# Four heads of attention on four row groups of TensorE, with 19 full-size matmuls as a bridge between projections and attention

## What is computed

```python
h = _layernorm(x) * (1 + ca) + sa
x = x + ga * attention(h)        # 16 heads of 8, rotary q and k, k and v from a latent of 64
h = _layernorm(x) * (1 + cb) + sb
x = x + gb * ffn(h)              # 4 rounds, each: top 2 of 4 experts, 128 -> 512 -> 128, gelu
```

```python
scores = jnp.einsum('bqhd,bkhd->bhqk', q, k) * scale
allowed = pages[None, :] <= pages[:, None]          # pages of 32 tokens
attn = jax.nn.softmax(jnp.where(allowed, scores, finfo.min), axis=-1)
out = jnp.einsum('bhqk,bkhd->bqhd', attn, v)
```

## Time and profile before

| | |
|---|---|
| time, median of 3 runs (lowest, highest) | 771.92 us (769.81 to 772.23) |
| time of the profiled execution | 771.94 us |
| its span, instructions | 770.1 us, 12222 |
| PE matmul busy | 681.2 us (88%) |
| DVE busy | 588.5 us (76%) |
| ACT busy | 520.4 us (68%) |
| POOL busy | 183.8 us (24%) |
| mean granted clock of PE | 0.94 |

### The profile page before, as it was taken

The page is one execution under the profiler, slowest core; times in us unless marked ns, Lnnn a source line. Parts: engine busy times, 40 slices in busy tenths (PEclk is TensorE's granted clock), DMA queues, the critical chain, the costliest instruction groups (busy, mean ns, idle before and its releaser), DMA issues.

```text
span 770.1 us, 12222 instructions
## 1 busy us (share of the span) xinstructions
PE 681.2 (88%) x3976; PEld 427.2 (55%) x4000; DVE 588.5 (76%) x1133; ACT 520.4 (68%) x905; POOL 183.8 (24%) x144
## 2 busy tenths in 40 slices
PE   3920988999699999987599999999999999999996
PEld 2410222333233333345478777787777877778885
DVE  5670987888588888229678898888988889888775
ACT  2530035677476777973488888888888888888984
POOL 0451016000000000000223343333433344322322
PEclk9965579999899999998799999999999999999998
DMA  9541041100101000000111110011100111101200
GB/s 237 150 139 65 0 117 40 43 21 25 46 2 44 24 20 4 3 1 1 66 45 55 56 56 28 29 56 56 55 34 24 54 56 57 54 2 55 69 15 28
DMA packets 17413, 37.20 MB, mean 48 GB/s; under 512 B 3305, under 2 KB 11241, under 8 KB 14533
## 3 DMA queue, kind: packets, MB, share of 16 engines
q1 hardware_dynamic: 16037, 34.65, 13.9%
q10 hardware_dynamic: 1312, 1.74, 0.9%
HBM read 31.86 MB, written 4.33 MB: 47 GB/s over the span
## 4 chain that ended last, share of the span: by engine, by line
PE 33%; DVE 12%; issue 5%; ACT 1%; POOL 0%; POOLq 0%; DVEq 0%
DVE gel_lo L1049 6%; PE y L952 6%; PE y L954 5%; PE y L953 5%; PE hid L943 5%; PE hid L942 5%; PE hid L941 5%; PE plog L963 2%; DVE part L1105 1%; ACT gel_hi L1017 1%; DVE at_least L1077 1%; PE pcw L972 1%; DVE cw L1096 0%; DVE cw L1094 0%; DVE dl L1084 0%
## 5 line engine op out<-in xcount | busy, mean ns | idle before, releaser
L1049 DVE TENSOR_TENSOR gel_lo<-gel,gel_hi 128x512 fp32r<-128x512 f32 x256 | 248.3, 1010 | 6.7 <-ACT gel_hi L1017 5.7
L588 DVE TENSOR_REDUCE mcol<-mx 128x1 f32<-128x512 f32 (+2 forms) x320 | 193.1, 635 | 61.7 <-PE mx L704 58.8
L562 ACT ACTIVATE probs<-st 128x512 f32<-128x512 f32 x288 | 155.7, 596 | 99.3 <-PE st L660 57.1
L1016 ACT ACTIVATE gel<-hid,b_sb 128x512 f32<-128x512 f32 x256 | 176.1, 688 | 38.5 <-PE hid L943 16.2
L1017 ACT ACTIVATE gel_hi<-hid,b_sb 128x512 fp32r<-128x512 f32 x256 | 174.7, 682 | 0.0
L1157 POOL TENSOR_TENSOR cur<-cur,part 128x512 f32<-128x512 f32 x64 | 106.4, 1663 | 250.8 <-DVE part L1105 250.8
L704 PE MATMUL mx<-ks,qs 125*128 125x512 bf16 (+3 forms) x384 | 120.8, 364 | 38.3 <-PEq L208 32.0
L952 PE MATMUL y<-gel_hi,w_hi 128*128 128x512 f32 x256 | 104.4, 408 | 0.4 <-DVE gel_lo L1049 0.2
L941 PE MATMUL hid<-cur_hi,w_hi 128*128 128x512 f32 x256 | 102.2, 399 | 0.4 <-DVE cur_lo L1123 0.4
L943 PE MATMUL hid<-cur_hi,w_lo 128*128 128x512 f32 x256 | 102.2, 399 | 0.0
L942 PE MATMUL hid<-cur_lo,w_hi 128*128 128x512 f32 x256 | 102.1, 399 | 0.0
(11 more groups left out here) (147 smaller groups left out, 521.9 us busy)
## 6 DMA issues: line engine op xcount, KB each, us to landing
cwb<-gate_rows SPq DMA_DIRECT2D x16, 1024.0 KB, 4.7
ks<-in_k_rows SPq DMA_DIRECT2D x3, 640.0 KB
qs<-in_q_rows SPq DMA_DIRECT2D x3, 616.0 KB
q_pieces<-pieces_q SPq DMA_DIRECT2D x4, 384.0 KB, 4.8
k_pieces<-pieces_k SPq DMA_DIRECT2D x4, 384.0 KB, 6.0
ks<-k_pieces SPq DMA_DIRECT2D x8, 192.0 KB
qs<-q_pieces SPq DMA_DIRECT2D x8, 192.0 KB
x_sb<-in_x SPq DMA_DIRECT2D x4, 256.0 KB, 5.2
```

The costliest lines, as they stand in the source:

```text
L562: nc.scalar.activation(probs[u % SLOTS][:, h, :], st[:, (HG * u + h) % ST_RING, :], ACT.Exp, scale=SCALE).then_inc(exp_done, 1)
L588: nc.vector.tensor_reduce(mcol[a % SLOTS][:, h, slot:slot + step * (len(blocks) - 1) + 1:step], mx[:, at % MX_RING, 0:len(blocks) * keys]. ...
L1016: nc.scalar.activation(gel[n % RING][:, :], hid[n % RING][:, :], ACT.Gelu_apprx_tanh, bias=bias)
L1049: nc.vector.tensor_tensor(gel_lo[n % RING][:, :], gel[n % RING][:, :], gel_hi[n % RING][:, :], ALU.subtract).then_inc(lo_ok, 1)
```

## The change

q and k are kept as float32r in two pieces, and three products (`Q_PIECE`, `K_PIECE`) are summed: 24 rows, two for the maxima, four for the page mask of the tile on the diagonal. So a head takes 30 rows of the 32 of a row group (`HROWS`), and the four heads of a group stand on the four row groups of one tile `ks`, `qs` [128, 1024]. The mask rows are used only in a matmul of its own for the 128 columns on the diagonal, so many matmuls are split in two. The tables of constant rows are written to DRAM beside the pieces.

A bin now holds two heads in two banks (`PAIRS` = 2), and one reduction of DVE reads both: 20 pairs a group; `mx` has two slots. The maxima have two pieces, cut by POOL. `ov` has one bank. A group has 10 units, two of them of 256 columns, and `weigh` isn't cut in halves. The loop is written out.

`BUSY_PREP` = 19 float32 matmuls stand behind prep's work on PE, and `keep_busy` puts 5, 2 or 1 float32r matmuls of full size, whose results nobody reads, ahead of pairs of bins.

```diff
+BUSY_PREP, BUSY_RISE, BUSY_FIRST, BUSY_LATER = 19, 5, 2, 1
...
 def load_group(sp, m, g, s):
-    for first, n in LOADS:
-        rows = slice(first * D, (first + n) * D)
-        sp.dma_start(m.ks[s][rows, :, :],
-                     m.kp[0:n, g].rearrange("c (d h) t -> c d (h t)", d=D)).then_inc(m.qk_in[s], 16)
-        one = m.qp[Q_PIECE[first]:Q_PIECE[first] + 1, g].rearrange("c (d h) t -> c d (h t)", d=D)
-        sp.dma_start(m.qs[s][rows, :, :], one.broadcast_to([n, D, HG * T])).then_inc(m.qk_in[s], 16)
+    for dst, src in ((m.ks[s], m.kp), (m.qs[s], m.qp)):
+        sp.dma_start(dst[:, :].bitcast(F32), src[g].rearrange("h r t -> (h r) t")).then_inc(m.qk_in[s], 16)
...
+            pe.wait_ge(h_ok, NCH)
+            for i in range(BUSY_PREP):
+                nc.tensor.matmul(turned[i % 2][:, :], m.ident[:, :], m.x[:, 0:TPC, :], start=True, stop=True)
...
-    ST_RING, MX_RING = 3, 3
+    ST_RING, PROBS, MX_RING = 3, 3, 2
...
-    ov = l.ps("ov", [P, 2, CH])
-    mx = l.ps("mx", [P, MX_RING, CH])
+    ov = l.ps("ov", [P, CH])
+    mx = l.ps("mx", [P, MX_RING, PAIRS, CH])
...
+            def keep_busy(g, n):
+
+                at = bin_at(g, n)
+                first = PAIRS * (NU + LEAD)
+                count = BUSY_RISE if at < 2 * PAIRS else BUSY_FIRST if NBINS * g + n < first else BUSY_LATER * (n % PAIRS == 1)
+                for i in range(count):
+                    nc.tensor.matmul(mx[:, at % MX_RING, i % 2, :], m.ks[g % SLOTS][:, 0:P], m.ks[g % SLOTS][:, 0:CH],
+                                     start=True, stop=True)
...
+            for unit in range(NU + LEAD):
+                for pair in range(PAIRS):
+                    bins(unit, pair)
+            for k in range(STEPS):
+                scores(k, 0)
+                scores(k, 1)
+                bins(k + NU + LEAD, 0)
+                scores(k, 2)
+                if k >= 1:
+                    weigh(k - 1)
+                bins(k + NU + LEAD, 1)
+                scores(k, 3)
+            weigh(STEPS - 1)
```

More of the change, by code:

```diff
@@ L72 @@
 ]
[L73 to L75 removed]
+PAIRS = HG // 2
+NBINS = len(BINS) * PAIRS
 LEAD = 4
[L77 to L80, removed]
+TURN_AFTER = 2 * PAIRS
+BUSY_PREP, BUSY_RISE, BUSY_FIRST, BUSY_LATER = 19, 5, 2, 1
 class Mem:
@@ L288, in _ @@
                 for side in range(2):
[L289 to L301, removed]
+                    pool.wait_ge(piece0, 2 * c + side + 1)
+                    nc.gpsimd.tensor_tensor(pieces[side][:, c, 1, :], ro[side][:, c % 2, :], pieces[side][:, c, 0, :],
+                                            ALU.subtract).then_inc(piece1, 1)
         @block.vector
@@ L516, in _ @@
             sp.dma_start(m.tri[:, :, :, :], m.w["tri"]).then_inc(small_in, 16)
-            all_groups(sp, body)
+            load_group(sp, m, 2, 2)
+            for g in range(GROUPS):
+                max_rows(g)
+                if g >= 1 and g + 2 < GROUPS:
+                    sp.wait_ge(st_done, HG * NU * g)
+                    load_group(sp, m, g + 2, (g + 2) % SLOTS)
             sp.wait_ge(small_in, 112)
@@ L578, in _, with exps @@
-            exps(0, 0, 0)
-            all_groups(act, body)
+            def exps(k, h):
+                u = k % NU
+                n = sum(b[3] for b in UNITS[u][1])
+                act.wait_ge(st_done, HG * k + h + 1)
+                if h == 0 and k >= PROBS:
+                    act.wait_ge(pv_done, k + 1 - PROBS)
+                nc.scalar.activation(probs[k % PROBS][:, h, 0:n], st[:, (HG * k + h) % ST_RING, 0:n], ACT.Exp,
+                                     scale=SCALE).then_inc(exp_done, 1)
@@ L651, in _, with scores @@
+            for g in range(GROUPS):
+                for n in range(NBINS):
+                    if n == 1 and g >= 1:
+                        merge(g - 1)
+                    if n == TURN_AFTER and g >= 1:
+                        keep_rows(g - 1)
+                    read_bin(g, n)
+            merge(GROUPS - 1)
+            keep_rows(GROUPS - 1)
         @block.tensor
         def _(pe):
-            def scores(i, a, u, h):
-                s, n = a % SLOTS, HG * (NU * gnum(i, a) + u) + h
+            def scores(k, h):
+                g, u = divmod(k, NU)
+                s, n, r0 = g % SLOTS, HG * k + h, HROWS * h
+                c, blocks = UNITS[u]
@@ L724, in body @@
-            def body(i, a):
-                for u in range(NU):
-                    nxt, side = following(i, a, u), part_at(i, a, u)
-                    for half in range(2):
-                        if exists(*nxt[:2]):
-                            scores(*nxt, 2 * half)
-                            scores(*nxt, 2 * half + 1)
-                        if exists(*side[:2]):
-                            part(*side, 2 * half)
-                        weigh(i, a, u, half)
-                        if exists(*side[:2]):
-                            part(*side, 2 * half + 1)
-                    if side[2] == 0 and exists(i, a + 1) and not exists(*side[:2]):
-                        turn_maxima(i, a + 1)
@@ L740, in _ @@
[L740 to L750 removed]
+                    own = P if k0 + keys == (t + 1) * P else 0
@@ new lines, in fill_bin @@
+                    for rows, y, w in ((ROW_MAX, 0, keys - own), (ROW_END, keys - own, own)):
+                        for i in range(PAIRS):
+                            r0 = HROWS * (2 * pair + i)
+                            if w:
+                                mm = nc.tensor.matmul(mx[:, at % MX_RING, i, x * keys + y:x * keys + y + w],
+                                                      m.qs[s][r0:r0 + rows, t * P:(t + 1) * P],
+                                                      m.ks[s][r0:r0 + rows, k0 + y:k0 + y + w], start=True, stop=True)
```

426 lines of the change are left out of this document (171 added, 255 removed).

## The result

The changed kernel takes 917.77 us (median of 4 runs, 912.96 to 920.12), the kernel before 772.08 (4 runs, 769.81 to 774.68): a ratio of 1.188, with a 95% interval of 1.181 to 1.194. It is slower by 146 us. The forecast was 781, its range 755 to 803.

What follows compares the result with a forecast made beforehand. Narrow transfers were taken to bound the pause, DVE the lead, PE the loop, then a ring of waits after the change. Start -13.1, loop +19.3 and lead +3.2 gave +9.4 on 771.92 us: forecast 781, range 755 to 803.

Steps and rivals of the forecast that it cites:

- The clock falls: Rival for lead and loop: row-grouped matmuls may not hold the full clock; 804 us or more, chance 0.08.
- the bridge: Full-size matmuls, 19 after prep and more before pairs of bins, expected to hand the attention a full clock.
- the loop: The attention's 8 groups from the first scores on, 107 to 341 us before; forecast +19.3 us.
- The ring: Loop's closed wait: score 2, weighing, bridge, bins, score 3, exponential, each turn awaiting the last; 3.28 us a unit.
- a group 32.9 us: Loop: eight full and two small units, split scores and the single `ov` bank make 32.9 us, against 29.2.
- score 2: Ring's first term, a score matmul waiting for the previous unit's last exponential: 0.06 + 0.31 us.
- score 3: Ring's last score matmul, for which the unit's last exponential waits: 0.24 us.
- Prep and pause: Stretch before the attention: transfers over 128 rows let bins start at 62.3 us, 13.1 us earlier.
- the common one: Prep's bridge: of two profiled times per float32 matmul, 0.96 and 0.86 us, the forecast took 0.96.
- The lead: Bins before the first scores: 28 pairs replace 57 bins, 34.8 us against 31.6, so +3.2.
- Faster, 757: Rival for the ring: cheap bridge switches and weights loaded ahead take up to 0.49 us off; chance 0.27.
- Row groups overlap less: Rival for loop and lead: queued weight loads give 798 us, no overlap 819; chance 0.15.

Runs made afterwards that it cites:

- old_rows32: Kernel before the change, with scores and bins contracting rows 0 to 31 alone, number and columns of matmuls kept; 928.2 us.
- rows128: Changed kernel with all scores and bins contracting 128 rows instead of 32, mixing the heads; 796.8 us.
- nobusy: Changed kernel without any bridging matmul, neither after prep nor in the attention; 871.6 us.
- scores_rows128: Changed kernel with only the scores contracting 128 rows, the bins keeping row groups of 24 and 30 rows; 848.0 us.
- three_pieces: As wide_rows_flat, but DRAM keeps the three bf16 pieces of each row once, loads again of 24, 16 and 8 partitions; 751.11 us, ratio 0.974.
- zeros_in_rows: Changed kernel with 128 rows per score and bin, other heads' rows zero in each head's query copy, page mask left out; 801.2 us.
- wide_rows_flat: Kernel before with rows laid out for loads onto 48 partitions and the loop over groups written out; 757.23 us, ratio 0.980.

## Why the prediction was wrong

**The clock is the step that failed.** The costs of PE's pieces were taken "all at the full clock", and against *The clock falls* stood two reasons: 107 matmuls of 128 columns that kept it at 1.00, and the bridge. The 107 (a count of records, and some of the matmuls leave two) are short matmuls, and all of them have 128 rows. What changed here was the height, and for that the forecast had no row. The bridge did hand over the full clock, and the attention had lost it 33 us later. The chance of 0.08 was too small; the clause beside it, "in the loop the loss would be over 100 us", gives the size right: the loop lost 149.4. old_rows32 shows the rows to be enough by themselves to hold the clock down, and rows128 that with 128 rows it does not fall in the changed kernel.

**The loop, but for the clock.** The ring was worked out as 3.28 us and is 3.32 in the turn shown at the full clock, whose bins are split and not of 512 columns. The row groups do overlap as the forecast had it: at 253.44 the matmuls of two heads, 512 columns each, take 0.79 us together, and one alone takes 0.79 at 255.03. The Trainium skill (TensorE: Matmul & The Clock Gate, Part 3) has row tiles run side by side; the trace agrees, with that 0.79. The step "a group 32.9 us" could not be seen, since no whole group ran at 1.00.

**Where a group's 51.65 us come from.** Predicted 32.9, ring-bound. At half the clock the columns of the ring double: score 2 0.24, weighing 0.86, bridge 0.24, bins 0.24 and score 3 0.24 more, 1.8 us a full unit and half of it or so in a small one: an estimate of 32.9 + 8 x 1.8 + 2 x 1.2 = 49.7 from the terms of the forecast. The remaining 2 us were not worked out. Weight loads are longer too (0.29 us ahead of the bridging matmul at 252.71, 0.19 at 124.62).

**Prep and pause.** Forecast 13.1 us earlier, measured 16.0. The bridge began at 42.26 and not at 43.43. The transfers were done by about 59 (15.0 us at 324 GB/s, where 344 was taken), and the 19 matmuls took 0.87 us each (16.58 for 38 halves), not 0.96: the lower of the two rows, not the common one. That both end together was right (0.3 us apart, by nobusy).

**The lead.** Forecast +3.2, measured +7.8. The clock, at 0.50 for the last 6.9 us, seems the smaller part: rows128 has 1.00 there and still takes 38.0 (59.48 to 97.46), for the changed kernel's 39.4, though its bins do not overlap. The term that was too small is the bridging inside the lead: without it, and at 0.50 all through, nobusy takes 30.8, less than the 31.6 of before. The forecast put its price at 6.8, as 34.8 less the 28 that DVE alone needs; it was 8.6, against a lead at half the clock.

**Rivals.** *Faster, 757* is out: a ring of 3.32 leaves nothing of its 0.49. *Row groups overlap less* is out by the timeline. The FFN kept its length but for 2.6 us, of which the clock may be the cause (0.81 from 480 to 500 us, 1.00 from 340 to 360 in the kernel before); this was not tried.

**What stays open.** What makes the same code run at one level and later at the other: the changed kernel's loop at 0.99 from 122 to 142.9 us, that of scores_rows128 at 1.00 from about 190. Whether two row groups at work at once count together towards the clock was not separated: scores_rows128 still mixes both. And no run shows a row-grouped loop at 1.00 for a whole group, so what the change would give with a full clock is only worked out, near the 781 of the forecast.

## What to carry to other kernels

Before packing short contractions into row groups, ask what holds TensorE's clock: a trace with the same busy share and columns but full rows says nothing about it, and a run of the old kernel with fewer rows costs one edit and shows it. Padding the contraction with zeros to 128 rows can be faster (801 against 918 us) than using the rows alone. Price matmuls that are put in for the clock alone by a run without them: here that run was 46 us faster. Take a change apart that has two halves: here the layout of the transfers, with the loop written out, was worth some 20 us in the old attention, and the other half cost that many times over.

## What was not expected of the hardware

- The level of the clock is not given by busy time: 0.97 busy with 32 or 64 rows ran at 0.50, 0.95 busy with 125 and 128 rows at 1.00 (three_pieces). Nor do the rows alone give it: the lead of before has 125 rows, is busy 0.91 and stands at 0.50. The Trainium skill (TensorE: Matmul & The Clock Gate, Part 1) speaks of a monitor of PE's busy-ness; by busy time as the profile counts it, the trace of old_rows32 does not agree.
- Rows that hold zeros count as rows: 1.00 in zeros_in_rows.
- With scores at 128 rows and bins at 24 to 30, the same loop ran at 0.50 until about 190 us and then at 1.00 to its end.
- Loads in rows of 2 KB onto 48 partitions moved at 157 GB/s with the DMA engines busy 0.98 (wide_rows_flat, 50 to 60 us). The length of written rows hardly mattered: rows of 1 KB at 364 GB/s there, rows of 2 KB at 383 in the changed kernel.
